# Half of a stack's DMA issues moved from SyncE's queue to ScalarE's, with new order lists on every engine

## What is computed

```python
h = _rmsnorm(x, gamma1)
q = (h @ Wq + bq).reshape(b, t, H, HD)
kv = ((h @ Wdown + bdown) @ Wup + bup).reshape(b, t, H, 2 * HD)
k, v = jnp.split(kv, 2, axis=-1)
att = jax.nn.softmax(jnp.einsum('bthd,btgd->bthg', q, k) / np.sqrt(HD), axis=-1)
x = x + (jnp.einsum('bthg,btgd->bthd', att, v).reshape(b, t, D) @ Wo + bo)
h2 = _rmsnorm(x, gamma2)
gate = jax.nn.softmax(h2 @ Wg + bg, axis=-1)
return x + jnp.einsum('btd,edf,bte->btf', h2, We, gate)
```

## Time and profile before

| | us |
|---|---|
| median of 3 runs | 2760.3 |
| lowest and highest run | 2759.11 and 2760.59 |
| the profiled execution | 2758.6 |
| its span in the profile | 2756.5 |
| PE busy (matmuls) | 2586.4 (94%) |
| DVE busy | 2133.6 (77%) |
| ACT busy | 1531.3 (56%) |
| POOL busy | 948.9 (34%) |
| DMA packets, MB | 845322, 119.29 |

### The profile page before, as it was taken

How to read it: one execution, slowest core, us unless ns; L and a number is a source line. 1 busy time by engine, 2 the same in 40 slices (tenths; PEclk the granted TensorE clock), 3 DMA queues, 4 the chain that set the end, 5 groups by cost and what they waited for, 6 DMA issues and landing times.

```text
span 2756.5 us, 48625 instructions
## 1 busy us (share of the span) xinstructions
PE 2586.4 (94%) x18896; PEld 1580.4 (57%) x18896; DVE 2133.6 (77%) x3647; ACT 1531.3 (56%) x2799; POOL 948.9 (34%) x970
## 2 busy tenths in 40 slices
PE   2458999999999999999999999999999999999999
PEld 2345566666556666655666665566666556655554
DVE  6677887788888778788877878887787888767743
ACT  5875555555555555555555555556555555654540
POOL 0453433333333333243333324333332433332420
PEclk7768999999999999999999999999999999999999
DMA  7202222211222221122222112222112222201220
GB/s 229 39 12 39 47 47 47 32 27 37 47 47 47 47 30 28 38 47 47 47 47 25 33 38 47 47 47 47 23 33 40 47 47 47 46 12 37 39 32 16
DMA packets 845322, 119.29 MB, mean 43 GB/s; under 512 B 813587, under 2 KB 813715, under 8 KB 845075
## 3 DMA queue, kind: packets, MB, share of 16 engines
q1 hardware_dynamic: 845092, 116.18, 22.9%
HBM read 48.49 MB, written 16.78 MB: 24 GB/s over the span
## 4 chain that ended last, share of the span: by engine, by line
PE 88%; DVE 4%; ACT 4%; POOL 2%; SPq 1%; issue 1%; DMA 0%; ACTq 0%; DVEq 0%; POOLq 0%
PE bank L1333 78%; PE bank L1355 3%; PE bank L1500 2%; PE bank L1471 2%; PE bank L1511 2%; DVE h2t L1104 1%; PE bank L1487 1%; POOL w_e L693 1%; ACT h2t L939 1%; PE bank L1512 1%; ACT ot L789 1%; DVE mcol L1234 0%; ACT t L888 0%; POOL pr L734 0%; DVE acc L1311 0%
## 5 line engine op out<-in xcount | busy, mean ns | idle before, releaser
L1333 PE MATMUL bank<-w_e,h2t 128*128 128x512 f16 x6144 | 1383.4, 380 | 2.8 <-DVE acc L1311 2.0
L1333 PEld LDWEIGHTS bank<-w_e,h2t 128*128 128x128 f16 x6144 | 592.1, 98 | 665.9 <-issue 4.4
L1311 DVE SCALAR_TENSOR_TENSOR acc<-bank,gates,acc 128x512 f32<-128x512 f32 x512 | 371.9, 736 | 120.4 <-PE bank L1333 117.4
L906 ACT ACTIVATE pr<-bank,plog,col 128x512 f32<-128x512 f32 x256 | 198.7, 776 | 407.9 <-PE bank L1500 405.5
L734 POOL TENSOR_TENSOR pr<-pr 128x512 f16<-128x512 f32 x256 | 295.7, 1160 | 182.3 <-ACT pr L908 180.9
L721 POOL TENSOR_TENSOR qo<-t,qo 128x256 f16<-128x256 f32 x128 | 106.5, 832 | 493.4 <-ACT qo L891 490.3
L1142 DVE TENSOR_TENSOR_SCAN wkv<-e,wkv 128x256 f32<-128x256 f32 x256 | 210.8, 864 | 74.6 <-ACT e L834 73.4
L1166 DVE RECIPROCAL zz<-zz 128x256 f32<-128x256 f32 x128 | 218.9, 1732 | 29.4 <-POOL zz L703 29.3
L1333 PE MATMUL bank<-w_o,xo 128*128 128x512 f16 x768 | 176.2, 387 | 46.9 <-DVE xo L1104 46.9
L908 ACT ACTIVATE pr<-bank,plog,col 128x512 f16<-128x512 f32 x256 | 197.8, 773 | 0.0
L1333 PE MATMUL bank<-xo,w_k 128*128 128x256 f16 x1536 | 172.9, 273 | 2.4 <-DVE xo L1104 2.4
(11 more groups left out here) (196 smaller groups left out, 3957.6 us busy)
## 6 DMA issues: line engine op xcount, KB each, us to landing
qs<-qo SPq DMA_DIRECT2D x384, 64.0 KB, 2.4
ks<-k SPq DMA_DIRECT2D x384, 64.0 KB, 2.4
xk<-in_attn_x SPq DMA_DIRECT2D x32, 512.0 KB, 4.0
x<-in_attn_x SPq DMA_DIRECT2D x32, 512.0 KB, 3.7
result<-acc SPq DMA_DIRECT2D x32, 512.0 KB, 2.8
w_e<-in_ffn_We SPq DMA_DIRECT2D x7, 1024.0 KB, 12.9
qs<-in_attn_Wk SPq DMA_DIRECT2D x1, 1024.0 KB, 7.9
ks<-in_attn_Wr SPq DMA_DIRECT2D x1, 1024.0 KB, 10.0
```

The source lines that it names most:

```text
L906: nc.scalar.activation(pr[:, k % 2, :], att_bank[ATT_BANK["S", k]][:, :], ACT.Exp, bias=plog[:, 0:1], scale=colof["soft"])\
L1311: V.scalar_tensor_tensor(out=acc[:, s, :], in0=moe_bank[u % 2][:, :], scalar=gates[:, s, e:e + 1], in1=acc[:, s, :], op0=ALU.mult, op1=ALU ...
L1333: ins = nc.tensor.matmul(dst, left(a), right(b), start=(n == 0), stop=(n == last))
```

## The change

ACT gets a new step, `att_send(t, n)` with n = 0 and 1: it waits for its own high half of q and then issues four of the 64 KB DMAs into `qs` on ACT's queue. SP's `att_up` keeps the low half of q, then k: 16 transfers instead of 24. The semaphore's total is the same. `att_send` is entered in ACT's table of steps, and the HEAD, ORDER and TAIL lists of all engines are replaced. "..." marks what is left out. The lists that are not shown (PE_HEAD, DVE_TAIL, ACT_TAIL, POOL_HEAD, POOL_TAIL, SP_TAIL) hold the same steps in another order, some of them handed over to the neighbouring list, and ACT's have `att_send` 0 and 1 ahead of each `att_up`.

```diff
--- before.py
+++ after.py
 PE_ORDER = [
-    ("att_scores", 4, 3), ("moe", 7, 4), ("att_probs", 3, 3), ("att_scores", 5, 3), ("moe", 8, 4),
-    ("att_probs", 4, 3), ("att_scores", 6, 3), ("att_probs", 5, 3), ("att_scores", 7, 3), ("mix_project", 0, 2),
-    ("att_probs", 6, 3), ("att_probs", 7, 3), ("mix_turn", 0, 1), ("moe", 9, 4), ("mix_k", 0, 1), ("att_turn", 0, 2),
-    ("mix_v", 0, 1), ("att_latent", 0, 2), ("att_q", 0, 2), ("moe", 10, 4), ("att_up", 0, 2), ("moe", 11, 4),
-    ("moe", 12, 4), ("fin_project", 0, 3), ("moe", 13, 4), ("moe", 14, 4), ("moe", 15, 4), ("fin_turn2", 0, 3),
-    ("att_max", 0, 2), ("att_max", 1, 2), ("fin_gate", 0, 3), ("moe", 0, 3), ("att_max", 2, 2), ("att_max", 3, 2),
-    ("moe", 1, 3), ("moe", 2, 3), ("att_m", 0, 2), ("moe", 3, 3), ("moe", 4, 3), ("att_scores", 0, 2),
-    ("att_scores", 1, 2), ("moe", 5, 3), ("att_probs", 0, 2), ("att_scores", 2, 2), ("moe", 6, 3),
-    ("att_probs", 1, 2), ("att_scores", 3, 2), ("att_probs", 2, 2),
+    ("att_scores", 3, 3), ("moe", 7, 4), ("att_probs", 2, 3), ("att_scores", 4, 3), ("att_probs", 3, 3),
+    ("att_scores", 5, 3), ("moe", 8, 4), ("att_probs", 4, 3), ("att_scores", 6, 3), ("att_probs", 5, 3),
+    ("att_scores", 7, 3), ("mix_project", 0, 2), ("att_probs", 6, 3), ("att_probs", 7, 3), ("mix_turn", 0, 1),
+    ("moe", 9, 4), ("mix_k", 0, 1), ("att_turn", 0, 2), ("mix_v", 0, 1), ("att_latent", 0, 2), ("att_q", 0, 2),
+    ("moe", 10, 4), ("att_up", 0, 2), ("fin_project", 0, 3), ("moe", 11, 4), ("moe", 12, 4), ("moe", 13, 4),
+    ("moe", 14, 4), ("moe", 15, 4), ("fin_turn2", 0, 3), ("att_max", 0, 2), ("att_max", 1, 2), ("moe", 0, 3),
+    ("fin_gate", 0, 3), ("att_max", 2, 2), ("att_max", 3, 2), ("moe", 1, 3), ("moe", 2, 3), ("att_m", 0, 2),
+    ("moe", 3, 3), ("moe", 4, 3), ("att_scores", 0, 2), ("moe", 5, 3), ("att_scores", 1, 2), ("moe", 6, 3),
+    ("att_probs", 0, 2), ("att_scores", 2, 2), ("att_probs", 1, 2),
 ]
 PE_TAIL = [
-    ("att_scores", 4, 4), ("moe", 7, 5), ("att_probs", 3, 4), ("att_scores", 5, 4), ("moe", 8, 5),
-    ("att_probs", 4, 4), ("att_scores", 6, 4), ("att_probs", 5, 4), ("att_scores", 7, 4), ("mix_project", 0, 3),
...
+    ("att_scores", 3, 4), ("moe", 7, 5), ("att_probs", 2, 4), ("att_scores", 4, 4), ("att_probs", 3, 4),
+    ("att_scores", 5, 4), ("moe", 8, 5), ("att_probs", 4, 4), ("att_scores", 6, 4), ("att_probs", 5, 4),
...
 ]
 DVE_ORDER = [
-    ("att_max", 1, 3), ("moe_gate", 0, 4), ("moe", 0, 4), ("att_max", 2, 3), ("att_max", 3, 3), ("moe", 1, 4),
-    ("mix_sum", 1, 2), ("att_m", 0, 3), ("moe", 2, 4), ("mix_value", 1, 2), ("moe", 3, 4), ("mix_scan", 1, 2),
...
-    ("mix_rec", 1, 1), ("mix_gate", 0, 1), ("att_vt", 0, 2), ("moe", 11, 4), ("moe", 12, 4), ("mix_split", 0, 1),
-    ("att_vlo", 0, 2), ("fin_project", 0, 3), ("moe", 13, 4), ("mix_decay", 1, 1), ("moe", 14, 4), ("moe", 15, 4),
-    ("fin_turn2", 0, 3), ("att_max", 0, 2),
+    ("att_max", 0, 3), ("att_max", 1, 3), ("moe_gate", 0, 4), ("moe", 0, 4), ("att_max", 2, 3), ("att_max", 3, 3),
+    ("moe", 1, 4), ("att_m", 0, 3), ("moe", 2, 4), ("mix_sum", 1, 2), ("mix_value", 1, 2), ("moe", 3, 4),
...
+    ("mix_rec", 0, 1), ("mix_rec", 1, 1), ("mix_gate", 0, 1), ("moe", 10, 4), ("fin_project", 0, 3), ("moe", 11, 4),
+    ("moe", 12, 4), ("att_vt", 0, 2), ("moe", 13, 4), ("mix_split", 0, 1), ("mix_decay", 1, 1), ("moe", 14, 4),
+    ("moe", 15, 4), ("fin_turn2", 0, 3), ("att_vlo", 0, 2),
 ]
 DVE_HEAD = [
...
-    ("mix_scan", 0, 1), ("att_vt", 0, 0), ("att_vlo", 0, 0), ("mix_rec", 0, 1), ("mix_rec", 1, 1), ("mix_gate", 0, 1),
-    ("att_max", 0, 0), ("att_max", 1, 0), ("att_max", 2, 0), ("mix_split", 0, 1), ("mix_decay", 1, 1),
-    ("mix_sum", 1, 1), ("att_max", 3, 0), ("att_m", 0, 0), ("mix_value", 1, 1), ("mix_scan", 1, 1), ("mix_rec", 2, 1),
...
+    ("set_g", 0, -1), ("mix_gate", 0, 1), ("att_vlo", 0, 0), ("att_max", 0, 0), ("mix_split", 0, 1),
+    ("mix_decay", 1, 1), ("att_max", 1, 0), ("att_max", 2, 0), ("att_max", 3, 0), ("att_m", 0, 0), ("mix_sum", 1, 1),
+    ("mix_value", 1, 1), ("mix_scan", 1, 1), ("mix_rec", 2, 1), ("mix_rec", 3, 1), ("mix_gate", 1, 1),
...
 ]
 ACT_HEAD = [
-    ("set_decay", 0, -1), ("pre_norm", 0, 0), ("mix_turn", 0, 0), ("set_abs", 0, -1), ("set_k", 0, -1),
-    ("set_k", 1, -1), ("set_r", 0, -1), ("set_r", 1, -1), ("set_abs", 1, -1), ("set_abs", 2, -1), ("set_abs", 3, -1),
-    ("mix_k", 0, 0), ("mix_v", 0, 0), ("mix_exp", 0, 0), ("set_o1", 0, -1), ("set_o1", 1, -1), ("set_abs", 4, -1),
-    ("set_abs", 5, -1), ("set_abs", 6, -1), ("set_abs", 7, -1), ("set_abs", 8, -1), ("set_abs", 9, -1),
...
-    ("set_times", 6, -1), ("set_times", 7, -1), ("set_e1", 1, -1), ("mix_exp", 0, 1), ("set_times", 8, -1),
-    ("att_latent", 0, 0), ("att_q", 0, 0), ("set_e2", 0, -1), ("att_up", 0, 0), ("set_times", 9, -1),
-    ("set_e2", 1, -1), ("att_vt", 0, 0), ("set_e3", 0, -1), ("set_e3", 1, -1), ("mix_num", 0, 1),
-    ("set_times", 10, -1), ("set_times", 11, -1), ("set_e4", 0, -1), ("set_e4", 1, -1), ("mix_split", 0, 1),
...
+    ("set_decay", 0, -1), ("pre_norm", 0, 0), ("mix_turn", 0, 0), ("set_k", 0, -1), ("set_k", 1, -1),
+    ("set_abs", 0, -1), ("set_abs", 1, -1), ("set_r", 0, -1), ("set_abs", 2, -1), ("set_r", 1, -1),
+    ("set_abs", 3, -1), ("set_abs", 4, -1), ("set_abs", 5, -1), ("set_abs", 6, -1), ("set_abs", 7, -1),
+    ("mix_k", 0, 0), ("mix_v", 0, 0), ("set_abs", 8, -1), ("mix_exp", 0, 0), ("set_abs", 9, -1), ("mix_num", 0, 0),
+    ("set_abs", 10, -1), ("set_abs", 11, -1), ("set_o1", 0, -1), ("mix_split", 0, 0), ("set_abs", 12, -1),
...
+    ("att_latent", 0, 0), ("att_q", 0, 0), ("mix_num", 0, 1), ("att_send", 0, 0), ("att_send", 1, 0),
+    ("att_up", 0, 0), ("set_e1", 0, -1), ("set_e1", 1, -1), ("set_times", 5, -1), ("set_times", 6, -1),
+    ("set_e2", 0, -1), ("set_e2", 1, -1), ("set_times", 7, -1), ("att_vt", 0, 0), ("set_times", 8, -1),
+    ("set_times", 9, -1), ("set_e3", 0, -1), ("set_e3", 1, -1), ("set_times", 10, -1), ("set_e4", 0, -1),
+    ("mix_split", 0, 1), ("set_e4", 1, -1), ("set_times", 11, -1), ("set_times", 12, -1), ("set_e5", 0, -1),
+    ("set_e5", 1, -1), ("set_times", 13, -1), ("set_times", 14, -1), ("set_times", 15, -1), ("set_e6", 0, -1),
...
+    ("set_e7", 0, -1), ("set_e7", 1, -1), ("mix_num", 1, 1), ("att_scores", 2, 0),
 ]
 ACT_ORDER = [
-    ("att_scores", 0, 4), ("mix_num", 1, 3), ("att_scores", 1, 4), ("att_scores", 2, 4), ("att_scores", 3, 4),
-    ("att_scores", 4, 4), ("mix_split", 1, 3), ("att_scores", 5, 4), ("att_scores", 6, 4), ("att_scores", 7, 4),
-    ("pre_norm", 0, 2), ("mix_turn", 0, 2), ("att_norm", 0, 3), ("mix_k", 0, 2), ("fin_back", 0, 4),
-    ("att_turn", 0, 3), ("mix_v", 0, 2), ("mix_exp", 0, 2), ("att_latent", 0, 3), ("att_q", 0, 3), ("mix_num", 0, 2),
-    ("att_up", 0, 3), ("att_vt", 0, 3), ("mix_split", 0, 2), ("fin_square", 0, 4), ("fin_norm2", 0, 4),
-    ("fin_turn2", 0, 4), ("mix_exp", 1, 2), ("moe_gate", 0, 4), ("att_rest", 0, 3),
+    ("att_scores", 3, 4), ("mix_split", 1, 3), ("att_scores", 4, 4), ("att_scores", 5, 4), ("att_scores", 6, 4),
+    ("att_scores", 7, 4), ("pre_norm", 0, 2), ("mix_turn", 0, 2), ("att_norm", 0, 3), ("mix_k", 0, 2),
+    ("fin_back", 0, 4), ("att_turn", 0, 3), ("mix_v", 0, 2), ("mix_exp", 0, 2), ("att_latent", 0, 3), ("att_q", 0, 3),
+    ("att_send", 0, 3), ("mix_num", 0, 2), ("att_send", 1, 3), ("att_up", 0, 3), ("mix_split", 0, 2),
+    ("att_vt", 0, 3), ("fin_square", 0, 4), ("fin_norm2", 0, 4), ("fin_turn2", 0, 4), ("moe_gate", 0, 4),
+    ("att_rest", 0, 3), ("mix_exp", 1, 2), ("att_scores", 0, 3), ("att_scores", 1, 3), ("mix_num", 1, 2),
+    ("att_scores", 2, 3),
 ]
-POOL_ORDER = [
-    ("att_stats", 0, 1), ("att_q", 0, 1), ("mix_sum", 0, 0), ("mix_num", 0, 0), ("att_up", 0, 1),
-    ("fin_square", 0, 2), ("moe_acc", 0, 2), ("att_rest", 0, 1), ("mix_sum", 1, 0), ("mix_num", 1, 0),
-    ("att_scores", 0, 1), ("att_scores", 1, 1), ("att_scores", 2, 1), ("att_scores", 3, 1), ("att_scores", 4, 1),
-    ("att_scores", 5, 1), ("pre_stats", 0, -1), ("att_scores", 6, 1), ("att_scores", 7, 1),
-]
+POOL_ORDER = [
+    ("att_scores", 3, 2), ("att_scores", 4, 2), ("att_scores", 5, 2), ("pre_stats", 0, 0), ("att_scores", 6, 2),
+    ("att_scores", 7, 2), ("att_stats", 0, 1), ("att_q", 0, 1), ("mix_sum", 0, 0), ("mix_num", 0, 0),
+    ("att_up", 0, 1), ("fin_square", 0, 2), ("moe_acc", 0, 2), ("att_rest", 0, 1), ("mix_sum", 1, 0),
+    ("mix_num", 1, 0), ("att_scores", 0, 1), ("att_scores", 1, 1), ("att_scores", 2, 1),
+]
 SP_HEAD = [
     ("pre_load", 0, 0), ("set_ident", 0, -1), ("set_load", 0, -1), ("set_load", 1, -1), ("set_load", 2, -1),
-    ("set_load", 3, -1), ("set_load", 4, -1), ("set_experts", 0, -1), ("set_experts", 1, -1), ("mix_k", 0, 0),
-    ("set_experts", 2, -1), ("set_experts", 3, -1), ("set_experts", 4, -1), ("set_experts", 5, -1),
-    ("pre_load", 0, 1), ("set_experts", 6, -1), ("set_experts", 7, -1), ("set_masks", 0, -1), ("mix_k", 0, 1),
```

(22 more changed lines are left out.)

296 lines of the change are left out of this document (146 added, 150 removed), and 2 rows, old and new, of the table POOL_HEAD.

## The result

The changed kernel takes 2830.6 us (median of 3 runs, 2830.40 to 2832.76) against 2760.3 us: a ratio of 1.0261, with a 95% interval from 1.0246 to 1.0276. The forecast was 2789.7 us with a range up to 2822; the sign was right, the size was not. The profiled execution has a span of 2828.3 us against 2756.5, so 71.8 us are to be found.

A forecast was written before the change was run, and what follows sets the result against it. The prediction took PE, 88% of the chain of waits, as the bound. From 2758.6 us it added 18.4 for the loop, 0.7 for PE_TAIL, 12 for the fill and 0 for the drain: 2789.7 us, range 2766 to 2822.

The forecast's parts named there:

- The place of moe 7: Loop, PE at att_probs(3): the new order makes PE wait 0.90 us an iteration; net 0.68 us, 18.4 us in all.
- The fill: Before the loop: the new head order on ACT delays tile 0's work; taken as +12 us, bounds 0 and +18.
- the 8 us for `set_abs` 4 to 7: Fill, ACT_HEAD: these calls ahead of mix_k wait for experts' weights, so k of tile 0 comes 8 us later.
- the experts' chain: Fill, ACT and POOL: six experts follow att_up of tile 0, ending near 174 us against 159: +15 us.
- The wait before the gate: Loop, PE waiting 0.74 us for h2's low half: it stays, now ahead of moe 0; cost 0.
- The eight issues on ACT: Loop, ACT's sends: 0.705 us each as on SP; the stack arrives 1.1 us later, still in time; cost 0.
- the 0.7 us of slack: Loop, PE at att_max: the stack lands at 1274.7 against att_max at 1275.40, leaving 0.7 us.
- Rival A: Loop, sends beside SP's low halves: ACT and SP take turns issuing, 1.4 us an iteration, 2828 us; chance 0.14.
- Rivals B and C: Fill, tile 0's attention: both large waits go, 2747.8 us (chance 0.11), or one goes, about 2759 us (chance 0.09).

The follow-up runs named there:

- orders-only kernel: The changed kernel with att_send taken out of ACT's lists and all 24 transfers back on SP: 2797.3 us, ratio 1.0139.
- sends-only kernel: The kernel before, old order lists, with ACT's two sends put in ahead of each att_up and SP left with 16 transfers: 2931.4 us, ratio 1.062.

## Why the sends are slow

**Nothing issued beside them.** SP's four low halves of q are moved behind all of k's transfers:

```diff
-                    sp.wait_ge(*att_pool.done(t, f"{name}_lo"))
...
+                low(k16, ks, 1)
+                low(qo16, qs, 2)
```

> The changed kernel with SP's four low halves of q moved behind all of k's transfers, so that SP issues nothing beside ACT's two sends. Theory (two queues that issue at once slow each other): ACT's first and second send take 2.8 us each, 5.6 us together instead of 7.6, and SP's four low halves 2.8 instead of 3.9. Rival (an issue on ACT costs 0.95 us by itself): the sends still take 7.6 us. The kernel's time is not the question: k comes 2 us earlier, and four issues (2.8 us) stand behind it, so that the stack is about 0.9 us later, 2840 to 2865 us.

Measured, on ACT:

```profile
1331.13 2.77 ACTq L887 DMA_DIRECT2D qs<-qo  x4
1333.97 2.81 ACTq L887 DMA_DIRECT2D qs<-qo  x4
```

An issue on ACT costs 0.70 us by itself, the value that I had taken; the other 2 us come from the second queue. (The one execution took 2907.5 us, more than expected. From ACT's first issue to the end of SP's last pass 21.4 us instead of 20.0, PE waits 3.2 us in the iteration shown, and the twelve matmuls behind that wait take 4.28 us: the lower clock again, which the expectation had left out.) The windows of the two bursts, this kernel's with ACT alone and the changed one's with both:

```profile
1331.50:1336.00 4.50, 4.50 (x30) 2.71 (x28) 3.57 (x5) 0.63 (x1) 3.23 (x3) 1.00 0.61 73
```

```profile
1293.20:1296.90 3.70, 3.70 (x24) 2.08 (x22) 2.78 (x4) 0.63 (x1) 2.55 (x2) 1.00 0.83 91
```

Two queues together move 91 GB/s, no more than SP's queue alone did in the earlier trace rows (94 GB/s). That a DMA locks the generator of descriptors for itself while they are made, as the Trainium skill has it (Perfetto Trace Analysis, "DMA Instruction — HWDGE"), fits but isn't separated here from the engines' own limit: they are busy 0.83 of the time.

**The sends kept, the overlap taken away.** SP waits until ACT's eight have landed before it issues the four; it has idle time there:

```diff
                     sp.wait_ge(*att_pool.done(t, f"{name}_lo"))
+                    if name == "q":
+                        sp.wait_ge(*stack_in.done(t, "qk", 7))
```

> The changed kernel with one wait added: SP issues q's four low halves only when ACT's eight transfers have landed; SP has idle time for them there, before k is ready. Theory (the two queues slow each other, and the 2 us that ACT loses put the stack behind att_max): the sends take 5.6 us, k comes 2 us and the stack 1.4 us earlier, the waits for ks and the stretches at half clock go, PE waits for h2's low half instead, an iteration is 81.5 to 81.6 us, 2806 to 2814 us, about the orders-only kernel plus what the sends cost in the fill. Rival (the stack is late however ACT's sends go): 2826 to 2835 us.

Measured: 2806.9 us, ratio 1.0172 (1.0155 to 1.0189). One added wait makes the changed kernel 24 us faster. SP's and ACT's issues follow each other now:

```profile
1449.74 2.77 ACTq L889 DMA_DIRECT2D qs<-qo  x4
1452.59 2.81 ACTq L889 DMA_DIRECT2D qs<-qo  x4
```

```profile
1458.83 2.79 SPq L664 DMA_DIRECT2D qs<-qo  x4
1461.67 5.67 SPq L658 DMA_DIRECT2D ks<-k  x8
```

The loop takes 2121.7 us, within 0.3 us of the orders-only kernel, and the drain 389.1. So all of the sends' price in the loop, and most of it in the drain, was the overlap of two queues. PE still waits for ks in some iterations (1.10 us in the one shown), but no more than the wait for h2's low half, or little more. In the fill 8.1 us against the orders-only kernel stay, 1.6 of them ahead of the first send. No run takes the rest apart; there ACT spends 5.8 us on the first eight issues ahead of k and of all its work behind.

## What the orders cost

**Only PE's middle put back.**

```diff
 PE_ORDER = [
-    ("att_scores", 3, 3), ("moe", 7, 4), ("att_probs", 2, 3), ("att_scores", 4, 3), ("att_probs", 3, 3),
+    ("att_scores", 3, 3), ("att_probs", 2, 3), ("att_scores", 4, 3), ("moe", 7, 4), ("att_probs", 3, 3),
...
-    ("att_scores", 0, 2), ("moe", 5, 3), ("att_scores", 1, 2), ("moe", 6, 3), ("att_probs", 0, 2), ("att_scores", 2, 2),
+    ("att_scores", 0, 2), ("att_scores", 1, 2), ("moe", 5, 3), ("att_probs", 0, 2), ("att_scores", 2, 2), ("moe", 6, 3),
```

> The changed kernel with the moe steps back among PE's scores and probs as before (scores 0, 1, moe 5, probs 0, scores 2, moe 6, probs 1, scores 3, probs 2, scores 4, moe 7, probs 3). Theory (moe 7 in the wrong place makes probs 3 wait for the chain scores 2 to p_lo 3): the gap of 0.72 us in the rows before probs 3 goes in every iteration, and 0.2 us before probs 5 with it, 0.2 us before probs 0 comes back: 0.9 us an iteration, 2803 to 2810 us. Rival (PE's place doesn't matter, as the stack's lateness takes up what is gained, being bound to ACT and SP): the gap goes but the wait for ks at att_max grows by as much, 2825 to 2831 us.

Measured: 2853.8 us, ratio 1.0339 (1.0323 to 1.0354): 23 us slower than the changed kernel, so both expectations failed. The gap before probs(3) is gone. Instead PE waits 0.30 us before probs(0) and 1.35 us before probs(2), for which DVE has to be done with probs(0):

```profile
1427.02 0.19 PE L1521 MATMUL bank<-vp,pr 128*128 128x66 f16 x1 [0.30 <-POOL pr L737]
1432.01 0.20 PE L1521 MATMUL bank<-vp,pr 128*128 128x66 f16 x1 [1.35 <-DVE on L1259]
```

```profile
1425.37 3.35 DVE L1176 RECIPROCAL zz<-zz 128x256 f32<-128x256 f32 x2
1428.65 0.65 DVE L1321 SCALAR_TENSOR_TENSOR acc<-bank,gates,acc 128x512 f32<-128x512 f32 x1
1429.21 1.67 DVE L1181 TENSOR_TENSOR ev<-ev,zz 128x512 f32<-128x512 f32 x1
1430.92 0.69 DVE L1185 SCALAR_TENSOR_TENSOR ev<-e,ev 128x512 f32<-128x512 f32 x1
1431.53 0.42 DVE L1259 TENSOR_REDUCE on<-bank 128x132 f32<-128x264 f32 x1
```

DVE's new list has mix_rec(2) and (3), moe 5 and mix_gate(1) ahead of probs(0), and PE's old order comes to probs(2) too early for it. (The expectation of the next run names moe 7, mix_split and pre_norm ahead of probs(4) for this; these rows show otherwise.)

**The middle put back on three engines.** Without sends, scores, probs and moe 5 to 8 in the old order on PE, ACT and DVE, with the mix and pre steps between them on DVE and ACT as they were (PE's part as above):

```diff
 ACT_ORDER = [
-    ("att_scores", 3, 4), ("mix_split", 1, 3), ("att_scores", 4, 4),
+    ("att_scores", 3, 4), ("att_scores", 4, 4), ("mix_split", 1, 3),
...
 DVE_ORDER = [
-    ("moe", 7, 4), ("mix_split", 1, 2), ("pre_stats", 0, 1), ("pre_norm", 0, 1), ("moe", 8, 4), ("att_probs", 4, 3),
+    ("att_probs", 4, 3), ("pre_stats", 0, 1), ("moe", 7, 4), ("moe", 8, 4), ("pre_norm", 0, 1),
...
```

> The orders-only kernel with the middle of the loop (scores, probs, moe 5 to 8) as before on all three engines: on PE a moe step between probs 2 and probs 3 again, on DVE and ACT the order that went with it. Theory (the new loop's loss of 0.94 us is the place of moe 7, and the loss on moving PE alone came from DVE's order, which then had moe 7, mix_split and pre_norm ahead of probs 4): the gap before probs 3 goes, an iteration is 80.6 to 80.8 us, 2770 to 2777 us. Rival (another wait takes its place whatever the middle is): 81.3 us or more an iteration, 2790 to 2800 us.

Measured: 2781.7 us, ratio 1.0084 (1.0069 to 1.0099), 15.5 us less than the orders alone, and nearly every iteration takes 80.88 us. So the new middle is the loss; that it is the place of moe 7 is argued from the gap before probs(3), which is gone, as the edit moves more than that step. The iteration is 0.1 us and the sum 5 us worse than expected: a gap of 0.30 us before probs(0) is left, one iteration takes 83.5 us, and the fill is 3.5 us longer than with the orders alone. These 3.5 us are not the edit's: the first product with xo, ahead of all that it moves, is 3.8 us later already (94.2 us against 90.4).

**The old HEAD lists**, first with the sends, then without:

```diff
 ACT_HEAD = [
...
-    ("set_abs", 3, -1), ("set_abs", 4, -1), ("set_abs", 5, -1), ("set_abs", 6, -1), ("set_abs", 7, -1),
-    ("mix_k", 0, 0), ("mix_v", 0, 0), ("set_abs", 8, -1), ("mix_exp", 0, 0),
+    ("set_abs", 3, -1), ("mix_k", 0, 0), ("mix_v", 0, 0), ("mix_exp", 0, 0), ("set_o1", 0, -1), ("set_o1", 1, -1),
...
```

> The changed kernel with the HEAD lists of before (with the sends put in for tile 0, and the few steps at their ends handed over so that they fit the new loop). Theory (the fill's 22 us are ACT's and POOL's new HEAD orders): mix_project of tile 0 starts near 82 us again, tile 2 reaches its mix_turn near 275 us, 2808 to 2815 us. Rival (the fill is long because of the sends and the new loop order right behind it): 2825 to 2832 us.

Measured: 2832.0 us, ratio 1.0265 (1.0249 to 1.028): nothing gained. Tile 0 reached its mix_turn at 103.5 us, as before, yet tile 2 only at 285.7 and tile 3 at 375.2 us, where the changed kernel is at 375.3: in old lists the sends cost the fill what the old lists give.

> The orders-only kernel with the HEAD lists of before: no sends anywhere. Theory (the 12.6 us by which the orders alone lengthen the fill are the new HEAD lists', ACT's set_abs ahead of the first mix_k among them; that old HEADs gained nothing with the sends in is the sends' doing, as they find no room in old lists): tile 0's mix_turn near 103.5 us, tile 2's near 272 us, 2784 to 2788 us. Rival (the fill's loss comes from the loop's first iterations, which the HEADs don't change): 2794 to 2800 us.

Measured: 2785.9 us, ratio 1.0099 (1.0084 to 1.0114), and tile 2 at 276.1 us. Of the orders' 12.6 us in the fill the HEADs are 8.4. The other 4.2 are not theirs: 2.3 stand already at tile 0's mix_turn (106.2 us against 103.9, in the old lists), within what fills differ by, and the rest comes with the loop's first turns. So the same edit is worth 11 us without the sends and nothing with them.

**Four calls of ACT_HEAD.** The orders-only kernel with `set_abs` 4 to 7 behind mix_v:

```diff
-    ("set_abs", 4, -1), ("set_abs", 5, -1), ("set_abs", 6, -1), ("set_abs", 7, -1), ("mix_k", 0, 0), ("mix_v", 0, 0),
+    ("mix_k", 0, 0), ("mix_v", 0, 0), ("set_abs", 4, -1), ("set_abs", 5, -1), ("set_abs", 6, -1), ("set_abs", 7, -1),
```

> The orders-only kernel with set_abs 4 to 7 behind mix_k and mix_v of tile 0 in ACT_HEAD, as before. Theory (those four calls wait for the experts' weights and hold back k of tile 0): PE's first w_o matmul with xo starts near 82 to 84 us instead of 92.4, tile 0's mix_turn near 104 us, and some 8 us of it lasts to the end, as with the old HEADs: 2786 to 2792 us. Rival (the experts' chain behind att_up sets the start of tile 0's attention anyway): the first w_o starts early, but tile 2 is where it was, 2794 to 2799 us.

Measured: 2787.2 us, ratio 1.0098 (1.0083 to 1.0113). These four calls are the HEADs' loss but for 1.2 us. PE's first product with xo, in the orders-only kernel and in this one:

```profile
90.40 7.89 PE L1340 MATMUL bank<-w_o,xo 128*128 128x512 f16 x24 [36.58 <-DVE xo L1111]
```

```profile
82.82 7.32 PE L1340 MATMUL bank<-w_o,xo 128*128 128x512 f16 x24 [45.62 <-DVE xo L1111]
```

## What in the orders carries the sends

**att_vt later on DVE**, in the sends-only kernel:

```diff
-    ("att_vt", 0, 2), ("moe", 11, 4), ("moe", 12, 4),
+    ("moe", 11, 4), ("moe", 12, 4), ("att_vt", 0, 2),
```

> The sends-only kernel with one step moved on DVE: att_vt behind moe 11 and moe 12 instead of ahead of them, as the changed kernel has it. Theory (in the sends-only kernel DVE stands 6.4 us at att_vt, waiting for v, which ACT copies only after the sends and k; moe 11's bank is drained late and PE waits 3 us ahead of moe 13): that wait goes, what is left is the stack's lateness of 0.6 to 1.4 us an iteration, 2785 to 2810 us. Rival (the loss is spread over all that ACT does later): 2880 us or more.

Measured: 2922.1 us, ratio 1.0587 (1.0571 to 1.0603). The theory failed in its size. DVE still waits 4.96 us at att_vt, and moe 13's bank is now the one that is drained late, as mix_split, att_vlo and fin_project come first; PE waits 2.69 us ahead of moe 15, and the lower clock follows: twelve matmuls behind that wait take 4.45 us instead of 2.75, and a row of 4.05 to 4.46 us stands in 25 of the 26 iterations.

**fin_project earlier as well**, as the changed kernel has it:

```diff
 PE_ORDER = [
-    ("att_up", 0, 2), ("moe", 11, 4), ("moe", 12, 4), ("fin_project", 0, 3), ("moe", 13, 4),
+    ("att_up", 0, 2), ("fin_project", 0, 3), ("moe", 11, 4), ("moe", 12, 4), ("moe", 13, 4),
 DVE_ORDER = [
-    ("att_vt", 0, 2), ("moe", 11, 4), ("moe", 12, 4), ("mix_split", 0, 1), ("att_vlo", 0, 2), ("fin_project", 0, 3), ("moe", 13, 4),
+    ("fin_project", 0, 3), ("moe", 11, 4), ("moe", 12, 4), ("att_vt", 0, 2), ("moe", 13, 4), ("mix_split", 0, 1), ("att_vlo", 0, 2),
```

> The sends-only kernel with fin_project moved two moe steps earlier on PE, and on DVE fin_project ahead of moe 11 and att_vt behind moe 12, mix_split behind moe 13, as the changed kernel has them; everything else as before. Theory (what the new orders do for the sends is to keep DVE from reaching att_vt and fin_project before ACT has copied v: in the run with att_vt alone moved, moe 13's bank was still drained behind att_vt, mix_split and fin_project): PE's waits for L1320 ahead of moe 15 go, an iteration is 81.2 to 82.4 us, 2780 to 2810 us. Rival (ACT is too late for everything in the old orders, att_scores included): over 84 us an iteration, 2880 us or more.

Measured: 2842.3 us, ratio 1.0307 (1.029 to 1.0324). An iteration takes 81.6 to 82.4 us, as expected, instead of 85.6, except the first, which takes 88.6 and has the only row at the lower clock. The sum was missed outside the loop's steady part: tile 2 comes at 286.5 us instead of 271.9, and the drain takes 415.0 us instead of 388.9. The HEAD and TAIL lists are the old ones without this room; that this is the reason wasn't run apart.

**Three mends at once**, sends kept: the overlap taken away, the old middle, `set_abs` behind.

> The changed kernel, sends kept, with three things mended at once: SP's low halves of q behind ACT's sends (as in the run that keeps them apart), the middle of the loop as before on PE, DVE and ACT, and set_abs 4 to 7 behind mix_v in ACT_HEAD. Theory (the three losses are separate and add up): 2807 less 16 for the middle and less 10 for set_abs, an iteration of 80.9 to 81.0 us, 2777 to 2785 us. Rival (in the old middle the sends cost more, as they did in the old orders): 2795 us or more.

Measured: 2785.3 us, ratio 1.0089 (1.0074 to 1.0104). The iteration is 80.88 us almost throughout. Taken singly, the three mends give 2781 us together, 4 less than this, so the losses add up nearly once the queues are apart. Against the kernel before 25 us are left, 10 in the fill and 14 in the loop; 0.3 us an iteration go with a gap of 0.30 us before probs(0), and two late iterations take some 83.6 us.

## Two attempts at the old loop's own wait

Before the gate PE idles 0.74 us by the bracket in the earlier trace rows. With fin_project and fin_turn2 each one moe step earlier, and then with fin_turn2 alone, on PE and DVE. The second edit, PE's part:

```diff
 PE_ORDER = [
-    ("moe", 15, 4), ("fin_turn2", 0, 3),
+    ("fin_turn2", 0, 3), ("moe", 15, 4),
```

> The kernel before, with fin_project one moe step earlier and fin_turn2 ahead of moe 15 instead of behind it, on PE and on DVE. Theory (the wait of 0.9 us for h2's low half ahead of the gate is the only idle time of the old loop, and ACT has h2's source ready in time): one moe step covers it, an iteration is 79.7 us, 27 of them save 24 us: 2733 to 2740 us. Rival (the source isn't ready, or DVE's work moved ahead of moe 15 delays a bank): PE waits in fin_turn2 or a moe step instead, 2755 to 2765 us.

Measured: 2796.2 us, ratio 1.0139 (1.0122 to 1.0156).

> The kernel before with fin_turn2 and moe 15 swapped on PE and DVE, and fin_project left in its place. Theory (moving fin_project broke DVE's order; h2's source is ready at 1271.6 where PE would start to turn it at 1271.9): one moe step covers the wait of 0.9 us ahead of the gate, 79.7 to 79.8 us an iteration, 2734 to 2740 us. Rival (DVE's fin_turn2 ahead of moe 15 waits and drains moe 15 or the maxima late, so that PE waits elsewhere): 2755 us or more.

Measured: 2795.1 us, ratio 1.0127 (1.0112 to 1.0142). Both kernels are 35 us or more slower than the one before, where 20 us less were expected. PE waits 1.12 us ahead of the gate in both, and the second shows why. ACT's and PE's timelines of the second:

```profile
1457.83 1.08 ACT L939 ACTIVATE h2t<-bank 128x512 f16<-128x512 f32 x2 [4.01 <-PE bank L1333]
```

```profile
1459.81 0.76 PE L1333 MATMUL bank<-w_g,h2t 128*128 128x8 f16 x24 [1.12 <-DVE h2t L1104]
```

ACT may write h2t only when PE has ended moe 15 of the tile before, which reads it (a wait at the head of ACT's `fin_turn2`). The turn was early, h2 was not, and DVE stood in the queue. The old order is at the limit that one buffer sets; a second one was not run. No kernel here is faster than the one before.

## Why the prediction was wrong

- **The place of moe 7: right.** 0.90 us were forecast at att_probs(3), 0.88 are lost by the neighbouring rows. Not foreseen was another 0.22 us before probs(5). Orders alone lose 0.99 us an iteration against the 0.68 forecast, 8 us over the loop.
- **The fill: right in size for the orders, in part by luck.** 12 us were taken; the orders alone cost 12.6. The first product with xo was put near 90 us and came at 90.4 (92.4 with the sends), and the 8 us for `set_abs` 4 to 7 were right: moving these alone back gives 8.5 us. But the text chose +12 by leaning to the experts' chain, on which its +15 rested, and by the HEADs' 8.4 us this chain adds next to nothing.
- **The wait before the gate: right** as long as the stack is in time; it moved to moe 0 with the same 0.74 us.
- **The eight issues on ACT: the step that failed.** The text took SP's 0.705 us each, the value of one queue alone, for issues that stand beside SP's own four. They cost 0.95 us each, 2.0 us more for the eight. As mix_num ran beside them and not behind, the stack's last issue began 19.26 us after the first send, where the text has 17.73: 1.5 us later. That is more than the 0.7 us of slack that the text counted, and it gave the step a cost of 0. With the slack gone, every longer block and late landing goes into PE's wait. By the spans the sends cost 18 us in the loop, and 16 in the fill and the drain, for which the sum had no term. By the medians they are 33 of the 41 us by which the forecast was short: 24 are the overlap, which one wait takes away; the other 9 lie mostly in the fill and stay unexplained. The rest of the 41 is the orders' 8 us in the loop.
- **Rival A** had the place and gave 2828 us, near the 2830.6 measured, and that nearness is luck: it put 38 us of the sends into the loop, where they cost 18. Its mechanism was half right: the two queues do take from each other, but a send lasts 2.9 to 5.2 us and not 5.64, and its cost is nothing in the best iterations (81.53 us with and without the sends, since the wait for h2's low half covers it) and up to 3.8 us in the worst (85.36), where longer issues and the lower clock come on top. It was given 0.14, on the ground that no row showed two queues at work; the row that spoke for it, 94 GB/s at a busy share of 0.78, was read as saying only that the second queue gains little, and not that it takes from the first.
- **Rivals B and C**, a fill shorter by one or both of its large waits, did not come: the fill is 21.8 us longer, and PE's wait for tile 0's stack is 18.3 us, where it was 18.7.

## What to carry to other kernels

A transfer moved to an idle queue is not priced by its row alone: if the other queue issues at the same time, take the burst's total as fixed, and see who is behind each issuer. Keep two queues apart in time where one of them has room; here one wait was worth 24 us. An order list on one engine is half of an edit: put back on PE alone it cost 23 us (with the sends), and on three engines it gained 16 (without them).

## What was not expected of the hardware

- Two queues with 64 KB transfers issued 12 in 7.6 us (0.64 each), against 0.70 each for either alone: a second queue brought a tenth.
- A single wait of 2 to 3 us on PE in a busy loop can be followed by some 3 us at the clock's lower level, which cost 1.6 us. In the changed kernel this came three times; four others, of 1.86 to 2.53 us, were not followed by it. In the sends-only kernel it makes up a third of the loss of the iteration shown.
- Single blocks of issues last 0.5 to 1.4 us longer now and then (6.80 instead of 5.58 us for eight on SP), and a last transfer lands up to 2 us later than most. Before, the slack hid the long blocks (up to 6.93 us there, with no wait of PE for the stack in the loop); in the changed kernel they go straight into PE's wait. What makes them long stays open.
